# Causal attention in one core's four-stage kernel: head stacks written by transfers within SBUF, two heads' scores in two row halves of TensorE

## The chip, the cores and the metric

The kernel runs on one core of one Trainium2 chip. The metric is the device time of one execution in microseconds (us), lower is better. TensorE (PE) multiplies, VectorE (DVE), ScalarE (ACT) and GpSimd (POOL) do the element work, and SyncE (SP) issues most of the transfers, which 16 DMA engines carry out.

## The reference, cut to what matters

Four layers follow each other, each with a layer norm before it and another before its sum with the residual: a Mamba-2 scan, a ternary feed-forward network, causal attention, and a mixture of eight experts. `x` is (2, 512, 512). Only the attention is touched:

```python
B, L, D, H = (32, 64, 512, 32)      # H = 32 heads of 16; b, l, d come from x: 2, 512, 512
q = (x @ Wq.T + bq).reshape(b, l, h, hd).transpose(0, 2, 1, 3)
k = (x @ Wk.T + bk).reshape(b, l, h, hd).transpose(0, 2, 1, 3)
v = (x @ Wv.T + bv).reshape(b, l, h, hd).transpose(0, 2, 1, 3)
scores = jnp.einsum('bhqd,bhkd->bhqk', q, k) / math.sqrt(hd)
causal = jnp.tril(jnp.ones((l, l), bool))
scores = jnp.where(causal, scores, -jnp.inf)
att = jax.nn.softmax(scores, axis=-1)
out = jnp.einsum('bhqk,bhkd->bhqd', att, v)
return out.transpose(0, 2, 1, 3).reshape(b, l, d) @ Wo.T + bo
```

The kernel keeps the accuracy of float32 by splitting operands into a high and a low part and adding the products of the parts.

## The kernel before, in words

The attention's heads are taken in 16 *quads* of four heads of one sequence. A *pair of quads* m (0 to 7) shares one projection: 128 rows of Q and of K, which are 8 heads. A quad has 8 *units*: four blocks of 128 queries (qi) times two head pairs (p2); there are 128 units, numbered n, and n%16 is the place of a unit within m. In unit n

- PE makes the scores of two heads (j = 0, 1) in two PSUM banks (L1933), and adds the causal mask by a bf16 product behind each (L1934), then signals `s_ready`;
- DVE takes the negated maximum of each row (L1504, `nmax`), ACT the exponential (L1169, `prob`);
- two units later PE transposes the probabilities (L1943), and ACT (L1161) and DVE (L1514) copy one head each into `pA` or `pB`;
- every half quad PE multiplies them by V (L1908); DVE copies the result (L1520, `osb`), PE transposes it back (L1954), DVE divides by the sums (L1530).

Scores are one product each because the parts of Q and K are stacked along the contraction: for a head 16 rows each of Q's high, low, high, low part stand against K's high, high, low, low part, 64 rows in all. Before, these stacks are made by PE: a selection matrix `selz` spreads the rows of `qh` and `ql` (L1887, L1888), ACT copies the Q stack from PSUM (L1144, `qs`), DVE the K stack (L1493, `kst`). One stack of 128 rows holds two heads, so POOL writes K twice, each time with the other head's 64 rows zeroed (L874, `kz`, by `head`), and a head's score contracts over all 128 rows. `qs` and `kz` have two buffers, for even and odd quads.

These preparations for the next quads are cut into *pieces*, hung behind fixed units by the function `pieces`: behind n%16 = 5, 6, 8, 9 six projection products each (L360, Q then K; bank 7), after 6 and 9 ACT makes the high part `qh` (L1136) and DVE the low part `ql` (L1485), and one stack behind each of 11, 12, 13, 14, 0, 1, 2, 3. Each engine runs its own list in the order in which it is written, so all that stands behind a waiting instruction waits too. SP issues next to nothing meanwhile: the reloads of Q and K weights, three in all (L569, L570), and at the stage's end the expert weights (L577).

Of the kernel before, what the change touches and what calls it, by code (L numbers as in the profile page):

```python
# [57 lines left out]
def program(nc, hidden, w_conv, w_gate, w_dt, conv_w, conv_b, dt_bias, A_log, Dskip, norm_w, w_out,  # L58
            ff_gu, ff_dn, gate_s, up_s, down_s, wq, wk, bqk, wv, bv, wo, bo, gate_w, expert_w, out):
    ctx = ExitStack()  # L60
    with ctx:
# [119 lines left out]
        kst = sc("kst", [P, 2, L], F32R)  # L181
# [6 lines left out]
        kz = sc("kz", [P, 2, 2, 2, L], F32R)  # L188
# [6 lines left out]
        selz = sc("selz", [P, 4, 4, P], F32R)  # L195
        abv = sc("abv", [P, DM])
        futf = sc("futf", [P, P])
        fold = sc("fold", [P, 2, HD])
        spare = sc("spare", [P, 352 + 4 * DM])
# [4 lines left out]
        head = sc("head", [P, 2])  # L204
# [22 lines left out]
        def sd(name, shape, dt=F32):  # L227
# [65 lines left out]
        qk_ps, qk_h, qk_l, st_ps, st_k, st_q, kpad = (sem(s) for s in (  # L293
            "qk_ps", "qk_h", "qk_l", "st_ps", "st_k", "st_q", "kpad"))
# [140 lines left out]
        def pieces(n):  # L435

            m, s = n // 16, n % 16
            for at, what in ((0, ("k", 0, 1)), (1, ("k", 1, 1)), (2, ("q", 0, 1)), (3, ("q", 1, 1))):
                if s == at:
                    return (m,) + what  # L440
            for at, what in ((5, ("proj", 0, 0)), (6, ("proj", 0, 1)), (8, ("proj", 1, 0)), (9, ("proj", 1, 1)),
                             (11, ("k", 0, 0)), (12, ("k", 1, 0)), (13, ("q", 0, 0)), (14, ("q", 1, 0))):
                if s == at and m + 1 < AT * NB:
                    return (m + 1,) + what
            return None
# [17 lines left out]
        ORDER = (("k", 0), ("k", 1), ("q", 0), ("q", 1))  # L463
        SEL = 9 + 8 + 2 + 4 * 8
# [17 lines left out]
        def _(sp):  # L482
# [72 lines left out]
            if STAGES >= 3:  # L555
# [10 lines left out]
                with sp.Fori(0, AT - 1) as t:  # L566

                    sp.wait_ge(aq_lo, 2 * t + 2)
                    sp.dma_start(aqr[:, 0, :, :], wq[bass.ds(t + 1, 1)]).then_inc(aq_in, 16)  # L569
                    sp.dma_start(aqr[:, 1, :, :], wk[bass.ds(t + 1, 1)]).then_inc(aq_in, 16)  # L570
            if STAGES >= 4:
# [9 lines left out]
                sp.wait_ge(st_ps, 4 * QUADS)  # L581
# [123 lines left out]
        def _(pool):  # L705
# [96 lines left out]
            if STAGES >= 2:  # L802
                norm_wait(pool, 1, "tr", NT)
                pool.memset(acc[:, :, :], 0.0).then_inc(consts, 1)
                if STAGES >= 3:
# [25 lines left out]
                    flat = fold[:, :, :].rearrange("p a b -> p (a b)")  # L831
                    made(pool.tensor_tensor(flat, ident[:, 0:32], ident[:, 32:64], ALU.add))
                    made(pool.tensor_tensor(flat, flat, ident[:, 64:96], ALU.add))
                    made(pool.tensor_tensor(flat, flat, ident[:, 96:128], ALU.add))
# [25 lines left out]
            if STAGES >= 3:  # L860
# [7 lines left out]
                def padded(quad, p2):  # L868

                    pool.wait_ge(st_k, 2 * quad + p2 + 1)  # L870
                    if quad >= 2:
                        pool.wait_ge(s_ready, 8 * (quad - 1))
# [1220 lines left out]
```

## Time and profile before

| | us |
|---|---|
| median of 3 runs (1709.1 to 1710.33) | 1710.32 |
| profiled execution, its own time | 1712.04 |
| its span, first to last instruction | 1710.3 |
| PE busy over the span | 1549.1 (91%) |
| DVE / ACT / POOL busy | 1222.2 / 826.1 / 945.8 |
| mean granted TensorE clock | 0.962 |

A busy share is an average over four layers with different limits; what counts for a change in attention is read from its stretch, some 1218 to 1520 us from the span's start. Matmul durations in the rows include the pipeline: in a run of them the distance between two starts, 0.23 us for 512 columns, is what each costs, not the 0.39 us that stand beside it. "issue" names idle time in front of an instruction that waited for nothing visible.

### The profile page before, as it was taken

The page shows a single profiled execution, that of the slowest core. Times are in us where ns is not written, and L with a number is a line of the kernel's source. Part 1 is how long each engine was busy: PE and PEld are TensorE (multiplying, and loading weights), DVE is VectorE, ACT ScalarE, POOL GpSimd, SP SyncE. Part 2 cuts the span into 40 slices and gives each one's busy share as a digit, 9 for nine tenths or more (in the row PEclk, how much of TensorE's full clock was granted, in tenths as well). Part 3 has the DMA queues.
Part 4 walks back from the last instruction along what each step waited for, and adds up shares of the span by engine and source line. Part 5 has one row for each costly group of instructions (what it writes and reads, how often), then busy time and mean ns, then how long its engine had stood idle before and what let it go on. Part 6 is the DMA issues. An engine that isn't in the chain of part 4 may idle for free.

```text
span 1710.3 us, 26565 instructions
## 1 busy us (share of the span) xinstructions
PE 1549.1 (91%) x8870; PEld 1215.7 (71%) x8870; DVE 1222.2 (71%) x2024; ACT 826.1 (48%) x1639; POOL 945.8 (55%) x861
## 2 busy tenths in 40 slices
PE   5899999999999999999999879996899999987791
PEld 3677877878778778778787657874567767666681
DVE  5778788778778787877887866567466677767525
ACT  3464554554555545455554423331276666663231
POOL 4367576676675766776756851007442344327544
PEclk9999999999999999999999889998899999997796
DMA  3111012021110110211101111221000000032435
GB/s 119 38 50 59 17 50 64 12 79 38 48 61 18 49 61 12 80 37 49 61 19 50 56 56 62 74 99 37 1 14 1 14 1 1 28 146 75 133 133 166
DMA packets 49498, 92.61 MB, mean 54 GB/s; under 512 B 8016, under 2 KB 32720, under 8 KB 44176
## 3 DMA queue, kind: packets, MB, share of 16 engines
q1 hardware_dynamic: 45744, 79.58, 14.4%
q0 software_dynamic: 3680, 12.06, 2.1%
q8 instruction: 44, 0.72, 0.2%
q14 instruction: 30, 0.25, 0.0%
HBM read 81.14 MB, written 10.49 MB: 54 GB/s over the span
## 4 chain that ended last, share of the span: by engine, by line
PE 59%; DVE 17%; POOL 8%; issue 7%; ACT 6%; DMA 3%; SPq 0%; POOLq 0%; DVEq 0%; ACTq 0%
PE banks L360 28%; PE banks L1666 6%; DVE tap L1237 4%; PE banks L1943 3%; PE banks L1803 3%; PE banks L1731 2%; PE banks L1908 2%; PE banks L1725 2%; PE banks L1696 2%; DMA x<-in_w_gate 2%; PE banks L1933 2%; POOL wol L365 2%; PE banks L1740 2%; DVE xbc L1243 1%; DVE acc L629 1%
## 5 line engine op out<-in xcount | busy, mean ns | idle before, releaser
L1237 DVE SCALAR_TENSOR_TENSOR tap<-banks,parg,tap 128x511 f32<-128x511 f32 (+2 forms) x288 | 215.0, 747 | 26.9 <-ACT tap L943 19.6
L723 POOL TENSOR_TENSOR am<-ah,upto 128x1024 fp32r<-128x1024 f32 x64 | 121.6, 1901 | 179.7 <-PE banks L1696 138.6
L874 POOL TENSOR_SCALAR kz<-kst,head 128x512 fp32r<-128x512 f32 x64 | 99.0, 1564 | 160.3 <-DVE kst L1493 160.3
L360 PE MATMUL banks<-xTh,wch 128*128 128x512 f32 x384 | 162.8, 424 | 5.2 <-DVE em L1343 3.7
L951 ACT ACTIVATE th<-tap 128x512 f32<-128x512 f32 x96 | 60.7, 632 | 215.0 <-DVE tap L1237 212.9
L360 PE MATMUL banks<-xTh,wcl 128*128 128x512 f32 x384 | 151.2, 394 | 0.0
L360 PE MATMUL banks<-xTl,wch 128*128 128x512 f32 x384 | 150.7, 393 | 0.0
L1169 ACT ACTIVATE prob<-banks,nmax 128x128 f32<-128x128 f32 (+3 forms) x256 | 121.6, 529 | 55.3 <-DVE nmax L1504 55.1
L1504 DVE TENSOR_REDUCE nmax<-banks 128x2 f32<-128x256 f32 (+3 forms) x128 | 104.7, 818 | 40.5 <-PE banks L1934 40.3
L723 POOL TENSOR_TENSOR am<-al,upto 128x1024 fp32r<-128x1024 f32 x64 | 122.1, 1908 | 0.0
L1343 DVE TENSOR_TENSOR em<-banks,gmask 128x1024 f32<-128x1024 f32 x64 | 78.2, 1221 | 49.8 <-ACT banks L992 48.9
L360 PE MATMUL banks<-xTh,wgh 128*128 128x512 f32 x256 | 107.5, 420 | 0.9 <-DVE tap L1237 0.5
L1943 PE MATMUL banks<-ident,prob 128*128 128x128 f32 x640 | 95.9, 277 | 10.6 <-DVE pB L1514 7.2
L360 PE MATMUL banks<-woh,ynTh 128*128 128x512 f32 x256 | 103.3, 403 | 0.0
L360 PE MATMUL banks<-woh,ynTl 128*128 128x512 f32 x256 | 101.2, 395 | 0.0
L360 PE MATMUL banks<-wol,ynTh 128*128 128x512 f32 x256 | 100.9, 394 | 0.0
L360 PE MATMUL banks<-xTh,wgl 128*128 128x512 f32 x256 | 100.7, 394 | 0.0
L360 PE MATMUL banks<-xTl,wgh 128*128 128x512 f32 x256 | 100.0, 391 | 0.0
L360 PEld LDWEIGHTS banks<-xTh,wch 128*128 128x128 f32 x384 | 72.6, 189 | 34.2 <-DVE em L1343 10.0
L1666 PE MATMUL banks<-xTh,gu 128*128 128x512 f32 x224 | 89.9, 401 | 6.2 <-DVE hidf L1432 6.1
L943 ACT ACTIVATE tap<-banks,parg 128x512 f32<-128x512 f32 x96 | 74.1, 772 | 43.6 <-PE banks L360 37.0
L1243 DVE SCALAR_TENSOR_TENSOR xbc<-th,tap 128x512 f32<-128x512 f32 x96 | 86.5, 901 | 5.4 <-ACT th L951 0.9
(290 smaller groups left out, 4393.1 us busy)
## 6 DMA issues: line engine op xcount, KB each, us to landing
x<-grownT SPq DMA_DIRECT2D x96, 128.0 KB, 4.8
x<-in_w_conv SPq DMA_DIRECT2D x7, 1536.0 KB, 6.5
x<-in_w_gate SPq DMA_DIRECT2D x8, 1024.0 KB, 4.9
x<-in_w_out SPq DMA_DIRECT2D x8, 1024.0 KB, 4.8
eraw<-in_expert_w SPq DMA_DIRECT2D x8, 1024.0 KB, 7.3
gur<-in_ff_gu SPq DMA_DIRECT2D x7, 1024.0 KB, 4.7
x<-in_hidden SPq DMA_DIRECT2D x16, 256.0 KB, 3.6
mates<-yd SPq DMA_DIRECT2D x8, 512.0 KB, 4.6
```

The costliest lines, as they stand in the source:

```text
L360: m = nc.tensor.matmul(o, a, b, start=first and n == 0, stop=last and n == len(terms) - 1)
L723: m = pool.tensor_tensor(am[:, part, :, :], a[:, i, :].bitcast(F32).unsqueeze(2).to_broadcast([P, HG, P]), upto[:, :].unsqueeze(1).to_broa ...
L874: m = pool.tensor_scalar(kz[:, quad % 2, p2, j, :], kst[:, p2, :].bitcast(F32), head[:, j:j + 1], None, ALU.mult)
L943: nc.scalar.activation(tap[:, q % 2, :], bk(CONV_BANKS[q % 2]), ACT.Identity, bias=parg[:, CT * KC + q:CT * KC + q + 1], scale=parg[:, KC ...
L951: nc.scalar.activation(th[:, :], tap[:, q % 2, :], ACT.Tanh).then_inc(tanh_ready, 1)
L1169: e = nc.scalar.activation(prob[:, n % 2, j, 0:kw], bk(2 * (n % 2) + j)[:, 0:kw], ACT.Exp, bias=nmax[:, n % 2, j:j + 1])
L1237: nc.vector.scalar_tensor_tensor(tap[:, q % 2, sh:L], bk(CONV_BANKS[q % 2])[:, 0:L - sh], parg[:, KC * q + k:KC * q + k + 1], tap[:, q % 2 ...
L1243: nc.vector.scalar_tensor_tensor(xbc[:, q, b * L:(b + 1) * L], th[:, :], 1.0, tap[:, q % 2, :], ALU.add, ALU.mult).then_inc(xbc_ready, 1)
L1343: nc.vector.tensor_tensor(em[:, s % 2, :, :], decayed, gmask[:, :].unsqueeze(1).to_broadcast([P, HG, P]), ALU.mult).then_inc(m_ready, 1)
L1504: nc.vector.tensor_reduce(nmax[:, n % 2, :], banks[:, 2 * (n % 2):2 * (n % 2) + 2, 0:kw], AX, ALU.max, negate=True).then_inc(max_ready, 1)
L1666: m = mat(bk(2 * w + ft), gu[:, k, ft, w, :], part[:, k, tok], start=(k == 0 and part is xTh), stop=(k == KT - 1 and part is xTl))
L1943: m = pe.transpose(bk(4 + j)[:, c * P:(c + 1) * P], prob[:, w % 2, j, c * P:(c + 1) * P], ident[:, :])
```

## The change

The stacks are no longer made on PE, ACT, DVE and POOL. SP writes them by transfers within SBUF: a transfer copies 16 rows of 512 float32 (32 KB) of `qh` or `ql` to their place in `qs` or `kz`. A quad needs 2 (Q, K) x 2 (p2) x 4 (parts) x 2 (heads) = 32 of them, all 16 quads 512. `kz` has no zeroed half; a score contracts over 64 rows, head j over rows 64j to 64j+63 of the array, the two heads' products stand next to each other, and the two mask products stand behind both. Since no selection matrix scales Q any more, ACT scales the Q weights and bias (`q_scaled`). The projections are cut into 8 pieces of 3 products, behind n%16 = 3 to 6 and 8 to 11. Two new waits hold the buffers: PE waits at a quad's first unit for `qk_in`, and ACT waits before it overwrites `qh` for all transfers of the pair of quads before.

```diff
         def pieces(n):
             m, s = n // 16, n % 16
-            for at, what in ((0, ("k", 0, 1)), (1, ("k", 1, 1)), (2, ("q", 0, 1)), (3, ("q", 1, 1))):
...
+            for w, at in ((0, (3, 4, 5, 6)), (1, (8, 9, 10, 11))):
+                if s in at and m + 1 < AT * NB:
+                    return m + 1, w, at.index(s)
...
-        SEL = 9 + 8 + 2 + 4 * 8
+        SEL = 9 + 4
+        STACK = 2 * 2 * 4 * 2
+        def stacked(quad):
+            return 16 * STACK * (quad // 2 + 1)
...
+                for m in range(AT * NB):
+                    for u in range(2):
+                        quad = 2 * m + u
+                        if quad >= 2:
+                            sp.wait_ge(s_ready, 8 * (quad - 1))
+                        for w in range(2):
+                            sp.wait_ge(qk_l, 2 * m + w + 1)
+                            for p2 in range(2):
+                                of = 32 * (2 * u + p2)
+                                for r, part in enumerate((qh, ql, qh, ql) if w == 0 else (qh, qh, ql, ql)):
+                                    for j in range(2):
+                                        row, at = of + HD * j, 64 * j + HD * r
+                                        sp.dma_start((qs, kz)[w][at:at + HD, quad % 2, p2, :].bitcast(F32),
+                                                     part[row:row + HD, w, :].bitcast(F32)).then_inc(qk_in[quad % 2], 16)
+                    t = m // NB
+                    if m % NB == 0 and t + 1 < AT:
+                        sp.wait_ge(aq_lo, 2 * t + 2)
+                        sp.dma_start(aqr[:, 0, :, :], wq[t + 1]).then_inc(aq_in, 16)
...
                 sp.wait_ge(v_f, NT)
-                sp.wait_ge(st_ps, 4 * QUADS)
+                for n in range(2):
+                    sp.wait_ge(qk_in[n], stacked(QUADS - 2 + n))
...
-                def padded(quad, p2):
-                    pool.wait_ge(st_k, 2 * quad + p2 + 1)
...
+                    nc.scalar.activation(aqr[:, 0, :, :], aqr[:, 0, :, :], ACT.Copy, scale=HD ** -0.5).then_inc(q_scaled, 1)
+                    act.wait_ge(q_scaled, t + 1 + (t > 0))
...
                 def high(m, w):
                     act.wait_ge(qk_ps, 2 * m + w + 1)
+                    if m:
+                        for u in range(2):
+                            act.wait_ge(qk_in[u], stacked(2 * (m - 1) + u))
...
-                def queries(quad, p2):
-                    act.wait_ge(st_ps, 4 * quad + 2 + p2 + 1)
...
-                def keys(quad, p2):
-                    dve.wait_ge(st_ps, 4 * quad + p2 + 1)
...
-                            pe.wait_ge(kpad, 2 * quad + 2)
-                            pe.wait_ge(st_q, 2 * quad + 2)
+                            pe.wait_ge(qk_in[quad % 2], stacked(quad))
...
                         for j in range(2):
-                            o = bk(2 * (n % 2) + j)
-                            kn = max(kw, 2 * P)
-                            mat(o[:, 0:kn], qs[:, quad % 2, p2, qi * P:kw], kz[:, quad % 2, p2, j, 0:kn], start=True, stop=False)
-                            m = mat(o[:, kw - P:kw], identb[:, :], future[:, :], start=False, stop=True)
+                            rows, kn = slice(64 * j, 64 * j + 64), max(kw, 2 * P)
+                            mat(bk(2 * (n % 2) + j)[:, 0:kn], qs[rows, quad % 2, p2, qi * P:kw], kz[rows, quad % 2, p2, 0:kn],
+                                start=True, stop=False)
+                        for j in range(2):
+                            m = mat(bk(2 * (n % 2) + j)[:, kw - P:kw], identb[:, :], future[:, :], start=False, stop=True)
```

Also gone are POOL's 38 small instructions that built `selz`, `fold` and `head` during the feed-forward layer.

In the list of SP after the change, the transfers of an even quad from the second pair of quads on (names: `qs` the Q stack, `kz` the K stack; x4 is four in a row):

```order
L576 DMA qs<-qh 16x512 [waits qk_l,s_ready]
L576 DMA qs<-qh 16x512
L576 DMA qs<-ql 16x512 x2
L576 DMA qs<-qh 16x512 x2
L576 DMA qs<-ql 16x512 x2
L576 DMA qs<-qh 16x512 x2
L576 DMA qs<-ql 16x512 x2
L576 DMA qs<-qh 16x512 x2
L576 DMA qs<-ql 16x512 x2
L576 DMA kz<-qh 16x512 [waits qk_l]
```

Fifteen more K transfers follow, then the odd quad's 32, all from the same `qh` and `ql`. Before, SP has nothing at this place.

On PE, a unit with the projection piece behind it (n%16 = 9), before:

```order
L1933 MATMUL banks<-kz,qs 128x256 [waits exp_ready]
L1934 MATMUL banks<-future,identb 128x128
L1933 MATMUL banks<-kz,qs 128x256
L1934 MATMUL banks<-future,identb 128x128
L1943 MATMUL banks<-ident,prob 128x128 [waits pt_a,exp_ready]
L1943 MATMUL banks<-ident,prob 128x128 x3
L1943 MATMUL banks<-ident,prob 128x128 [waits pt_v]
L1943 MATMUL banks<-ident,prob 128x128 x3
L360 MATMUL banks<-xTh,aqh 128x512
L360 MATMUL banks<-xTl,aqh 128x512
L360 MATMUL banks<-xTh,aql 128x512
```

and the same unit after:

```order
L1877 MATMUL banks<-kz,qs 128x256 [waits exp_ready]
L1877 MATMUL banks<-kz,qs 128x256
L1880 MATMUL banks<-future,identb 128x128 x2
L1889 MATMUL banks<-ident,prob 128x128 [waits pt_a,exp_ready]
L1889 MATMUL banks<-ident,prob 128x128 x3
L1889 MATMUL banks<-ident,prob 128x128 [waits pt_v]
L1889 MATMUL banks<-ident,prob 128x128 x3
L358 MATMUL banks<-xTh,aqh 128x512
L358 MATMUL banks<-xTl,aqh 128x512
L358 MATMUL banks<-xTh,aql 128x512
```

The masks moved behind the pair of scores, and three products follow where six did before (the other three of the six rows' worth stand behind another unit).

On ACT, around the high part of Q's next projection (n%16 = 6), after the change:

```order
L1150 ACTIVATE prob<-banks,nmax 128x512 [waits pt_ps,max_ready]
L1150 ACTIVATE prob<-banks,nmax 128x512 [waits pt_ps]
L1124 ACTIVATE qh<-banks,abqk 128x512 [waits qk_in1,qk_in0,qk_ps]
L1142 COPY pB<-banks 128x384 [waits pt_ps]
L1150 ACTIVATE prob<-banks,nmax 128x512 [waits pt_ps,max_ready]
```

Before, the third row is `L1136 ACTIVATE qh<-banks,abqk 128x512 [waits qk_ps]` at the same place; its wait has gained the transfers of both quads, and the copies and exponentials of the units stand behind it.

## Rows read from the trace of the kernel before

**Rows 1.** Busy time by stretch: us, busy (instructions) of each engine, clock, DMA share, GB/s.

```profile
1260.00:1295.00 35.00, 32.97 (x283) 24.28 (x281) 24.49 (x43) 23.97 (x54) 14.88 (x10) 1.00 0.05 16
```

**Rows 2.** ACT's high parts in the timeline: start us, us, engine, line, op, tiles.

```profile
1284.99 0.69 ACT L1136 ACTIVATE qh<-banks,abqk 128x512 fp32r<-128x512 f32 x1 [0.50 <-PE banks L360]
...
1463.97 0.69 ACT L1136 ACTIVATE qh<-banks,abqk 128x512 fp32r<-128x512 f32 x1 [0.50 <-PE banks L360]
```

**Rows 3.** Timeline of PE: a stack (0.57 us to the next start), and a unit's scores.

```profile
1302.59 0.50 PE L1887 MATMUL banks<-qh,selz 128*128 128x512 f32 x1
...
1303.16 0.39 PE L1933 MATMUL banks<-kz,qs 128*128 128x512 f32 x1
...
1316.70 0.40 PE L1933 MATMUL banks<-kz,qs 128*128 128x512 f32 x1
...
1316.94 0.23 PE L1934 MATMUL banks<-future,identb 128*128 128x128 bf16 x1
...
1316.98 0.48 PE L1933 MATMUL banks<-kz,qs 128*128 128x512 f32 x1
...
1317.37 0.82 PE L1943 MATMUL banks<-ident,prob 128*128 128x128 f32 x6
```

**Rows 4.** SP's transfers in the timeline: start us, us that SP was in it.

```profile
6.76 0.68 SPq L489 DMA_DIRECT2D par<-in_conv_w  x1
...
1138.17 0.43 SPq L562 DMA_DIRECT2D abo<-in_bo  x1
1138.65 0.45 SPq L563 DMA_DIRECT2D rw<-in_gate_w  x1
...
1271.50 0.33 SPq L569 DMA_DIRECT2D aqr<-in_wq  x1
1271.93 0.38 SPq L570 DMA_DIRECT2D aqr<-in_wk  x1
```

**Rows 5.** DMA issues of the page: tiles, count, KB each, median us from issue to landing.

```profile
xnd<-acc SPq DMA_DIRECT2D x8, 256.0 KB, 2.0
...
gus<-in_gate_s SPq DMA_DIRECT2D x1, 7.0 KB, 2.7
```

**Rows 6.** Timeline, odd quad's units 8 to 12: what leads to K's low part.

```profile
1250.02 0.36 PE L1933 MATMUL banks<-kz,qs 128*128 128x256 f32 x1
...
1255.21 0.48 PE L360 MATMUL banks<-xTh,aqh 128*128 128x512 f32 x1
...
1256.68 0.28 PE L1933 MATMUL banks<-kz,qs 128*128 128x256 f32 x1
...
1257.61 0.75 DVE L1485 SCALAR_TENSOR_TENSOR ql<-banks,abqk,qh 128x512 fp32r<-128x512 f32 x1 [1.42 <-ACT qh L1136]
...
1260.32 0.34 PE L1933 MATMUL banks<-kz,qs 128*128 128x384 f32 x1
```

**Rows 7.** Timeline of the first quad's start.

```profile
1220.28 0.75 DVE L1485 SCALAR_TENSOR_TENSOR ql<-banks,abqk,qh 128x512 fp32r<-128x512 f32 x1 [2.85 <-ACT qh L1136]
...
1224.88 0.75 DVE L1485 SCALAR_TENSOR_TENSOR ql<-banks,abqk,qh 128x512 fp32r<-128x512 f32 x1 [3.85 <-ACT qh L1136]
...
1233.71 0.55 PE L1933 MATMUL banks<-kz,qs 128*128 128x256 f32 x1 [2.36 <-POOL kz L874]
```

**Rows 8.** PE's weight loads where the tile's shape changes, in the timeline.

```profile
1318.12 0.59 PEld L1908 LDWEIGHTS banks<-pA,v 128*32 128x32 f32 x16 [0.17 <-issue]
...
1318.90 0.19 PEld L360 LDWEIGHTS banks<-xTh,aqh 128*128 128x128 f32 x1 [0.20 <-issue]
```

**Rows 9.** Busy time by stretch around the first quad's start, columns as in group 1.

```profile
1228.00:1230.00 2.00, 0.73 (x2) 0.30 (x2) 0.67 (x1) 0.51 (x1) 2.00 (x2) 0.89 0.00 0
1230.00:1232.00 2.00, 1.22 (x2) 0.50 (x2) 0.00 (x0) 0.66 (x2) 2.00 (x3) 0.50 0.00 0
...
1239.00:1240.00 1.00, 1.00 (x6) 0.64 (x4) 0.55 (x2) 0.76 (x3) 1.00 (x2) 0.60 0.00 0
```

**Rows 10.** The page's busy tenths of POOL in 40 slices of 42.8 us.

```profile
POOL 4367576676675766776756851007442344327544
```

More of the change, by code:

```diff
@@ L187, in program @@
         future = sc("future", [P, P], BF16)
-        kz = sc("kz", [P, 2, 2, 2, L], F32R)
+        kz = sc("kz", [P, 2, 2, L], F32R)
+        under_aqr = sc("under_aqr", [P, 2, 2, L])
         aqr = sc("aqr", [P, 2, KT, P])
@@ L866, in _ @@
                     low(pool, awl[:, k, :], awr[:, k, :], awh[:, k, :]).then_inc(aw_lo, 1)
-                def padded(quad, p2):
-                    pool.wait_ge(st_k, 2 * quad + p2 + 1)
-                    if quad >= 2:
-                        pool.wait_ge(s_ready, 8 * (quad - 1))
-                    for j in range(2):
-                        m = pool.tensor_scalar(kz[:, quad % 2, p2, j, :], kst[:, p2, :].bitcast(F32), head[:, j:j + 1],
-                                               None, ALU.mult)
-                    m.then_inc(kpad, 1)
-                for p2 in range(2):
-                    padded(0, p2)
                 for n in range(UNITS):
-                    piece = pieces(n)
-                    if piece and piece[1] == "k":
-                        padded(2 * piece[0] + piece[3], piece[2])
                     if n % 32 == 14 and n // 32 + 1 < AT:
@@ L1173, in _ @@
                         if piece:
-                            m, what, i, u = piece
-                            if what == "proj" and u == 1:
-                                high(m, i)
-                            if what == "q":
-                                queries(2 * m + u, i)
+                            m, w, part = piece
+                            if part == KT - 1:
+                                high(m, w)
                         if n % 32 == 14 and n // 32 + 1 < AT:
@@ L1535, in _ @@
                     if piece:
-                        m, what, i, u = piece
-                        if what == "proj" and u == 1:
-                            lows(m, i)
-                        if what == "k":
-                            keys(2 * m + u, i)
+                        m, w, part = piece
+                        if part == KT - 1:
+                            lows(m, w)
                 dve.wait_ge(wide_in, 32)
@@ L1914, in _ @@
                 for w in range(2):
-                    for part in range(2):
+                    for part in range(KT):
                         project(0, w, part)
-                for what, i in ORDER:
-                    stack(0, what, i, 0)
                 pe.wait_ge(v_f, NT)
@@ L1957, in _ @@
                     if piece:
-                        prepare(*piece)
+                        project(*piece)
                 for i in range(NT + 6):
```

75 lines of the change are left out of this document (11 added, 64 removed).

## The prediction, made before the changed kernel ran

> **What bounds the kernel now.** I read the busy time by stretch first. In the steady part of attention PE is busy 33.0 of 35 us at full clock, DVE and ACT some 24, POOL 15, and the transfers run at 16 GB/s [rows 1]: PE sets the pace and the transfer side is empty. Then the timeline, for the rhythm: the high part of Q's projection for m = 2 starts at 1284.99, that for m = 7 at 1463.97, so a pair of quads takes 178.98 / 5 = 35.8 us [rows 2], a unit 2.24. Last the list of transfers, because the change puts 512 instructions on an engine, SP, that issues next to none in this stage.
>
> **What goes.** A stack costs PE 0.57 us from its first start to the next instruction's [rows 3]. There are 64, so 8 x 0.57 = 4.6 us per pair of quads: were PE still the bound, a pair would take 31.2 us and the stage would lose 64 x 0.57 = 36 us. ACT's and DVE's 32 copies each and POOL's 64 multiplications go too; all three engines have room [rows 1], so I count these at nothing. The projection products stay 24 per pair, only spread.
>
> **What the transfers cost.** SP is in a transfer 0.43 to 0.45 us and starts the next 0.48 us later when they stand in a row (1138.17 to 1138.65); two in a loop start 0.43 apart; the first after a wait takes 0.33, and patterns with more dimensions 0.68 [rows 4]. None of these is 16 rows within SBUF. The new ones have the plainest pattern and stand in a row, so I take 0.47 and keep 0.33 and 0.68 as ends. A quad is then 32 x 0.47 = 15.0 us of issuing. To landing the nearest rows are 2.0 us for a transfer out of SBUF and 2.7 for 7 KB into it [rows 5]; I take 2.0 (bounds 1.5, a quarter below the nearest row, and 2.7). SP's mean load is thus 30 of 35.8 us, which would fit. What doesn't fit is the chain that the waits make:
>
> 1. The odd quad's last transfer lands. Only then may its first unit start, and only then may ACT write the next `qh`, in front of its copies and exponentials.
> 2. From the odd quad's first score to K's next low part. Before, units 8 to 12 take 1250.02 to 1260.32, 10.3 us [rows 6]; two pieces of six products (1.47 each, 1255.21 to 1256.68) and a stack leave them, four pieces of three (about 0.77 each) come, which gives about 10.0. ACT and DVE first do the held-up high and low part of Q (0.69 + 0.75, and their queues behind), 1.5 us. Behind unit 11's piece come high and low part of K: from the end of the piece at 1256.68 the same two took until 1258.36, 1.7 us [rows 6]. Sum 13.2. The even quad's 16 Q transfers (7.5 us, from about 1.5 us on) lie under this.
> 3. Then 48 transfers in a row, 16 of K for the even quad and 32 for the odd one: 48 x 0.47 = 22.6 us. The even quad runs beneath, and starts some us late.
> 4. Landing, 2.0 us, and the circle closes.
>
> That is 13.2 + 22.6 + 2.0 = 37.8 us per pair against 35.8, or 2.0 more. PE's 4.6 us are gone from its work and come back as waiting at the first unit of each even quad. There are 7 such circles: +14.0.
>
> **The start.** Q's first low part ends at 1221.03 [rows 7]. From there 32 transfers are issued without a gap (K's low part is ready at 1225.6, before its turn), to 1236.1, and land at 1238.1; the first score stood at 1233.71, behind POOL's padding [rows 7]. The odd quad lands 15.0 later, at 1253.1, where it began at 1250.02 [rows 6]: +3.1 at the point where the circles begin.
>
> **The score products.** Before, scores and masks of a unit with 512 columns take 0.67 us of PE: 0.24 to the mask, 0.04 to the second score, 0.39 from there to the end of its mask [rows 3]. If the two half-height products run at the same time, the second's own 0.32 goes. If the array must first empty when the tile's shape changes, each unit pays twice what weight loads pay where the shape changes now, 0.17 and 0.20 [rows 8]: with both, 0.72; with the emptying alone, 1.04. No row shows a product over 64 rows, so the bounds are -0.32 and +0.37 per unit, and I take +0.05, overlap and emptying, the value that uses both rows. On the path are only the four units of step 2, so 28 units: +1.4, bounds -9 and +10. (The Trainium skill, TensorEngine Tiling (Array Packing), Key Properties, speaks for and against: tiles run in parallel, and "Changing tiling mode (not just tile) drains the TensorE". By the first alone the sum would be some 9 us less, by the second alone 10 more. The 0.17 and 0.20 us agree with the second; no run here shows the first.)
>
> **The rest.** ACT's scaling of 128x512 (about 0.6) stands once in the feed-forward layer, at most +0.6, and three times where SP is what everybody waits for; taken as 0. The 38 small instructions on POOL go from the feed-forward layer, where POOL is busy a tenth of the time and less in slices 25 to 27 [rows 10]: 0. The expert loads wait for quad 15's landing in place of the last stack; that lies a whole quad, about 15 us, before the attention's end, time enough for the first five. SP's reloads of Q and K weights fall where it waits for `s_ready`.
>
> **Sum.** 14.0 + 3.1 + 1.4 = 18.5, on the profiled execution's own 1712.0: 1730.5. That execution is 1.7 above the median of the runs, 1710.3, so the median goes to about 1729, and I say 1730.
>
> **Rivals.**
> A, the transfers are hidden after all: faster. The place is step 3. The circle is 48c + 15.2 with c the time of an issue; it equals 35.8 at c = 0.43, and with the start's cost the whole breaks even at about 0.42. At c = 0.33, the row after a wait, it is 31.0, and PE's 31.2 rules: 7 x -4.6, with all 64 stacks -36, 1675; at c = 0.40 (34.4) it is 7 x -1.4, -1.4 at the start and +1.4 for the scores, 1701. For it: 16 rows may be quicker to issue than 128. Against: 16 KB (L563) and 256 KB (L562) took SP 0.45 and 0.43 [rows 4], so size hardly matters.
> B, the clock falls. After a sparse stretch (0.73 of 2 us busy) the granted clock went from 1 to 0.50, the 1.2 GHz level, and in 1239 to 1240 it was still at 0.60 on average, with PE busy all of it [rows 9]. The change puts a wait of some 4 us and thin units before each even quad. If PE then works 4 us at half clock each time, the even quad, whose 15 us of issuing have hardly any slack over PE's work, ends 2 us later: 7 x 2 = +14, 1744. For it: the same kind of gap did it once. Against: it needs the even quad on the path, and step 3 says SP is. (The Trainium skill, TensorE: Matmul & The Clock Gate, Part 1, has it that idleness throttles the clock to half and only renewed activity frees it; rows 9 agree. By that rule the time would be 1744.)
> C, an issue costs 0.68 as with the longer patterns: the circle is 32.6 + 15.2 = 47.8, +12.0 each, 84, and 64 x 0.21 = 13 more at the start: 1812 with the start's 3.1 and the scores' 1.4. For it: 512 unrolled issues in a row are unlike anything here. Against: the 0.68 rows have patterns with many short runs.
> D, the half-height products don't run side by side: that is the +10 bound, 1739, within the forecast's range.
>
> **Chances and range.** Forecast with D 0.58, B 0.22, C 0.08, A 0.12. A change below 0.2% of the time, 3.4 us, is what a measurement here can't tell from none. An issue of 0.44 to 0.50 moves the forecast by (7 x 48 + 64) x 0.03 = 12 us either way, the landing by -4 to +5, the scores by -9 to +10. Faster comes from A (0.10 of its 0.12), same from the low edge of the forecast and A's rest, 0.08, slower 0.82. For 8 in 10 I go from 1706 to 1772: B with a slow issue is in, C and most of A are out.
>
> **What would show it.** In the changed profile: SP starts its transfers 0.47 apart, 48 without a gap, and idles some 4 us before the even quad's K transfers; PE's first score of even quads waits for a DMA some 4 us; ACT's `qh` for Q waits for a DMA; those starts are 37.8 us apart; the second score of a unit starts well under 0.2 us behind the first, with about 0.2 idle around the pair. Wrong would be: PE without waits for transfers (A), clock 0.50 behind each even start (B), starts 0.68 apart (C). If the landing takes far over 2 us with a queue that is never empty, step 4 is what I have mis-sized.

## The result and the profile after

| | before | after |
|---|---|---|
| median (runs) | 1709.72 us (4) | 1814.03 us (4; 1806.01 to 1815.37) |
| profiled execution, its own time | 1712.04 | 1815.37 |
| span | 1710.3 | 1813.6 |
| ratio after / before | | 1.061, 95% interval 1.059 to 1.062 |

The change costs 104 us. The forecast was 1730 in a range of 1706 to 1772: right in its sign, wrong in its size. In the steady part of attention, PE was busy 33 of 35 us [rows 1]. The same stretch after (columns as in group 1), and then a line of the page of after: where the chain that ended last spent its time, by engine.

```profile
1260.00:1295.00 35.00, 27.57 (x200) 18.30 (x200) 17.09 (x29) 18.25 (x41) 2.49 (x2) 0.74 0.22 56
```

```profile
PE 49%; SPq 14%; DVE 13%; issue 7%; POOL 7%; ACT 5%; DMA 4%; POOLq 0%; ACTq 0%; DVEq 0%
```

Every engine that computes is less busy. SPq, SyncE inside its issuing instructions, is now 14% of the chain, where before SP had next to nothing to do in attention. All of these 14% are on one line, L576, the stack transfers. The page's group for the scores (idle time in front of them behind the last bar) and its row for a transfer name what PE waits for:

```profile
L1877 PE MATMUL banks<-kz,qs 64*128 64x256 f32 (+2 forms) x256 | 63.3, 491 | 91.9 <-DMA kz<-ql 89.2
...
qs<-qh SPq DMA_DIRECT2D x128, 32.0 KB, 2.0
```

89.2 us of waiting for the last K transfer, at 16 quad starts. The rhythm, against [rows 2], is in ACT's high parts (timeline: start, duration, instruction, idle time before it):

```profile
1260.43 0.69 ACT L1124 ACTIVATE qh<-banks,abqk 128x512 fp32r<-128x512 f32 x1 [6.91 <-DMA kz<-ql]
...
1309.22 0.69 ACT L1124 ACTIVATE qh<-banks,abqk 128x512 fp32r<-128x512 f32 x1 [5.64 <-DMA kz<-ql]
...
1552.14 0.69 ACT L1124 ACTIVATE qh<-banks,abqk 128x512 fp32r<-128x512 f32 x1 [4.37 <-DMA kz<-ql]
```

A pair of quads takes (1552.14 - 1260.43) / 6 = 48.6 us instead of 35.8, and the high part of Q waits for the transfers each time. The seven circles run from the odd quad's start at 1260.37 to the last odd quad's at 1600.57, 340.2 us; before, the same starts are 1250.02 [rows 6] and 1498.39, 248.4 us (timeline of PE, first before, then after):

```profile
1498.39 0.36 PE L1933 MATMUL banks<-kz,qs 128*128 128x256 f32 x1
```

```profile
1260.37 0.58 PE L1877 MATMUL banks<-kz,qs 64*128 64x256 f32 x2 [5.75 <-DMA kz<-ql]
...
1600.57 0.58 PE L1877 MATMUL banks<-kz,qs 64*128 64x256 f32 x2 [5.61 <-DMA kz<-ql]
```

That is 91.8 us for the circles, 10.4 for the later start, and 1.1 behind the last odd quad's start: 103.3, the whole difference of the spans.

One circle as the chain of waits tells it (start, us, what; the runs of SPq rows are cut):

```profile
1307.17 1.95 DMA kz<-ql
1309.22 0.70 ACT qh L1124
1309.94 0.75 DVE ql L1464
1310.70 1.13 DVE nmax L1474
1312.35 1.12 PE banks L1889 x4
1313.46 1.28 PE banks L358 x3
...
1323.39 0.76 DVE ql L1464
...
1324.72 0.59 SPq L576
...
1331.04 1.50 SPq L576
...
1355.76 1.94 DMA kz<-ql
1357.80 0.70 ACT qh L1124
```

It is the circle of the prediction, link by link: the odd quad's last landing lets Q's high part go, units 8 to 11 follow, then K's low part, then SP alone from 1324.17 to 1356.34, and the last landing. And SP's timeline in it (x4 is four transfers in a row):

```profile
1324.17 2.40 SPq L576 DMA_DIRECT2D kz<-qh  x4
1326.62 2.49 SPq L576 DMA_DIRECT2D kz<-ql  x4
1329.14 3.40 SPq L576 DMA_DIRECT2D kz<-qh  x4
...
1345.28 3.47 SPq L576 DMA_DIRECT2D kz<-qh  x4
...
1353.85 2.49 SPq L576 DMA_DIRECT2D kz<-ql  x4
```

Four transfers take 2.52 us from start to start (1326.62 to 1329.14), 0.63 each, where I had taken 0.47; and two of these groups are 0.9 us longer than the others.

### The profile page after: what moved, and what is told of

It is laid out like the page before. It is cut to its first block, busy times and chain, and to the rows that moved or that the text cites. A ratio compares the mean times of both kernels' runs of the same rounds, so it can differ in the third digit from the quotient of the medians.

```text
span 1813.6 us, 26583 instructions
## 1 busy us (share of the span) xinstructions
PE 1565.7 (86%) x8742; PEld 1206.3 (67%) x8742; DVE 1202.6 (66%) x1992; ACT 817.3 (45%) x1612; POOL 834.1 (46%) x759
## 4 chain that ended last, share of the span: by engine, by line
PE 49%; SPq 14%; DVE 13%; issue 7%; POOL 7%; ACT 5%; DMA 4%; POOLq 0%; ACTq 0%; DVEq 0%
PE banks L358 26%; SPq L576 14%; PE banks L1634 6%; DVE tap L1216 3%; PE banks L1771 3%; PE banks L1699 2%; PE banks L1693 2%; PE banks L1664 2%; DMA x<-in_w_gate 2%; POOL wol L363 2%; PE banks L1708 1%; DVE acc L642 1%; PE banks L1889 1%; POOL am L736 1%; DVE xbc L1222 1%
## 5 line engine op out<-in xcount | busy, mean ns | idle before, releaser
L1877 PE MATMUL banks<-kz,qs 64*128 64x256 f32 (+2 forms) x256 | 63.3, 491 | 91.9 <-DMA kz<-ql 89.2
L1889 PE MATMUL banks<-ident,prob 128*128 128x128 f32 x640 | 125.5, 333 | 18.3 <-DVE pA L1484 7.1
L363 POOL TENSOR_TENSOR aql<-aqr,aqh 128x512 fp32r<-128x512 f32 x8 | 10.0, 1273 | 252.1 <-ACT aqh L1076 252.1
L1877 PEld LDWEIGHTS banks<-kz,qs 64*128 64x128 f32 x256 | 28.1, 216 | 132.9 <-DMA kz<-ql 74.1
L1889 PEld LDWEIGHTS banks<-ident,prob 128*128 128x128 f32 x640 | 90.8, 175 | 27.9 <-DVE pA L1484 11.0
```

Source lines behind the costliest of these rows:

```text
L1877: mat(bk(2 * (n % 2) + j)[:, 0:kn], qs[rows, quad % 2, p2, qi * P:kw], kz[rows, quad % 2, p2, 0:kn], start=True, stop=False)
L1889: m = pe.transpose(bk(4 + j)[:, c * P:(c + 1) * P], prob[:, w % 2, j, c * P:(c + 1) * P], ident[:, :])
```

## Experiments

Two theories stood at first. *Issue*: SP's time per transfer sets the 48.6 us. *Clock*: the granted clock is 0.50 for some us around each quad's start (0.74 on the mean of 1260 to 1295), and PE, not SP, is late.

**m1_bursts. What an issue costs, by itself.** The kernel before, with bursts on SP where nobody waits for it:

```diff
+                for n in range(N):
+                    sp.dma_start(to[0][16 * (n % 8):16 * (n % 8) + 16, :] if n < 8 else to[1][16 * (n % 8):16 * (n % 8) + 16, :],
+                                 abo[16 * (n % 8):16 * (n % 8) + 16, :]).then_inc(wide_in, 16)
+                sp.wait_ge(wide_in, 32 + 16 * N * 1)
...
+                for n in range(N):
+                    sp.dma_start(to[n // 8][16 * (n % 8):16 * (n % 8) + 16, :],
+                                 hidden[16 * n:16 * n + 16, :]).then_inc(wide_in, 16)
```

N is 12, and each burst waits for the one before. The bursts are 16 x 512 within SBUF, 128 x 64 within SBUF, 16 x 512 from HBM, 32 x 512 within SBUF, 128 x 64 from HBM.

> The kernel before, with five bursts of 12 transfers on SP in the attention stage, where SP has nothing to do; each burst waits until the one before has landed. Bursts in order: (a) 16 rows x 512 within SBUF, (b) 128 rows x 64 within SBUF, (c) 16 rows x 512 from HBM, (d) 32 rows x 512 within SBUF, (e) 128 rows x 64 from HBM. Theory 1, the source decides: a transfer with both sides in SBUF costs SP 0.63 us, as in the changed kernel, and one from HBM 0.47 as in the rows of before: (a), (b), (d) 0.63, (c), (e) 0.47. Theory 2, the shape decides, 16 rows cost more than 128: (a), (c) 0.63, (b), (e) 0.47, (d) between. Theory 3, it is the long run of transfers and neither: all five 0.47. The time of the kernel stays at 1710 by all of them, unless the traffic within SBUF slows the engines.

Ratio 1.000 (0.999 to 1.001). SP's timeline of the five bursts, in their order:

```profile
1340.77 7.57 SPq L574 DMA_DIRECT2D spare<-abo  x12
1349.71 8.81 SPq L578 DMA_DIRECT2D spare<-abo  x12
1359.77 5.50 SPq L582 DMA_DIRECT2D spare<-in_hidden  x12
1366.68 8.09 SPq L586 DMA_DIRECT2D spare<-abo  x12
1376.17 5.57 SPq L590 DMA_DIRECT2D spare<-in_hidden  x12
```

7.57 / 12 = 0.63 us for the transfer of the change. The second and the fourth burst look dearer only because each holds one long issue (1.79 and 1.15 us, more on these below); their other transfers start 0.64 and 0.63 apart. The same shape from HBM takes 0.46, as my rows did [rows 4]: all of those came from HBM. Neither height nor size decides.

All five bursts end in SBUF, so m1 alone would allow "the source" as the cause. The kernel before has transfers out of SBUF into HBM, each right behind a wait:

```profile
1541.41 0.33 SPq L594 DMA_DIRECT2D xnd<-acc  x1
```

0.33 us is what one from HBM takes behind a wait [rows 4], while one within SBUF takes 0.51 to 0.59 there (after). So it is having both ends in SBUF that costs, not the source alone.

**m2_half. Half the issues.** One transfer of 32 rows for both heads, 16 per quad (the scores then mix the two heads' parts and are wrong; number and shapes of all products stay).

```diff
-                                    for j in range(2):
-                                        row, at = of + HD * j, 64 * j + HD * r
-                                        sp.dma_start((qs, kz)[w][at:at + HD, quad % 2, p2, :].bitcast(F32),
-                                                     part[row:row + HD, w, :].bitcast(F32)).then_inc(qk_in[quad % 2], 16)
+                                    sp.dma_start((qs, kz)[w][32 * r:32 * r + 32, quad % 2, p2, :].bitcast(F32),
+                                                 part[of:of + 32, w, :].bitcast(F32)).then_inc(qk_in[quad % 2], 16)
```

> The changed kernel with half the transfers: 32 neighbouring rows (both heads) go in one, 16 per quad instead of 32, the same bytes. The rows of the stacks stand in another order, so the scores are those of mixed heads; the work is the same. Theory A, the time lies in the number of issues on SP and in the chain of waits that they stand in: the circle is 24 x 0.65 + 2.0 + 13.2 = 30.8 us per pair of quads, less than PE's 31.2 + 0.4, so PE sets the pace again: -4.2 us per pair against before, 8 x -4.2 = -34, some 1677 (1670 to 1692). Theory B, the time lies in the bytes within SBUF or in the landing: 64 KB take twice as long, nothing is won, 1800 or more.

1695.29 us, ratio 0.992 (0.990 to 0.994): 119 us faster than after, and 14 faster than before. The bytes are the same, so the number of issues is the cause of the loss. But it isn't the 1677 that PE's bound of 31.2 us per pair promised.

**m3_qh2. `qh` and `ql` twice**, so that the high part doesn't wait for the transfers of the pair before it.

```diff
-                    if m:
+                    if m > 1:
                         for u in range(2):
-                            act.wait_ge(qk_in[u], stacked(2 * (m - 1) + u))
+                            act.wait_ge(qk_in[u], stacked(2 * (m - 2) + u))
```

> The changed kernel with two buffers of qh and ql by turns, so that ACT waits for the transfers of the pair of quads before the last only. All 32 transfers per quad stay. Theory A (chain): the closed circle of 48.6 us per pair opens, and what is left is SP's own load, 64 x 0.63 + 2.7 for the longer ones = 43.0 us: 7 x -5.6 = -39, some 1775. Theory B (SP's load alone sets the pace already, the wait of ACT costs nothing): no change, 1814.

1795.37 us, ratio 1.050 (1.047 to 1.052), a miss by 20. ACT's high parts of Q, four pairs apart:

```profile
1302.01 0.69 ACT L1126 ACTIVATE qhs<-banks,abqk 128x512 fp32r<-128x512 f32 x1
...
1486.76 0.69 ACT L1126 ACTIVATE qhs<-banks,abqk 128x512 fp32r<-128x512 f32 x1
```

46.2 us per pair: 64 issues of 0.63 are 40.3, SP still waits 3.4 per pair for K's low part (24.0 us in seven waits), its long issues add 1.7, and the weights' reloads are most of the rest. With the circle opened SP's plain load remains above 35.8: two buffers don't save this change.

**m4_warm and m14_warm2. The clock.** The kernel after, with products that nobody reads ahead of the wait at a quad's start (20; then 24), and in the second kernel 6 more within the odd quad's first unit.

```diff
+                            if n:
+                                for i in range(20):
+                                    mat(bk(2 * (n % 2) + i % 2), awh[:, i % KT, 0:P], xTh[:, i % KT, 0:L], start=True, stop=True)
                             pe.wait_ge(qk_in[quad % 2], stacked(quad))
```

```diff
+                            if j and n % 16 == 8 and n // 16 + 1 < AT * NB:
+                                pe.wait_ge(qk_l, 2 * (n // 16) + 3)
+                                for i in range(6):
+                                    mat(bk(7), awh[:, i % KT, 0:P], xTh[:, i % KT, 0:L], start=True, stop=True)
```

> The changed kernel with 20 products of 512 columns (some 4.3 us at full clock) into the unit's own score banks in front of PE's wait for the transfers at each quad's start but the first; they are overwritten by the scores. Theory A, the clock that falls in the waits (0.50 for some 8 us after each quad's start) is part of the loss: the clock stays at 1, the way from the odd quad's start to K's low part falls from 15.0 to 13.2 us, 7 x -1.8 = -13, some 1801. Theory B, the slow stretches lie beside SP's issuing and cost nothing: 1814 within 3.

> The kernel after with products whose result nobody reads, in two places: 24 before the wait at each quad's start, and 6 in the odd quad's first unit between the transposes of its two heads, where TensorE idled 1.3 us in the run with 20 fillers and its clock then fell to 0.50, the 1.2 GHz level, until some 3 us later. So that run had only moved the fall, not removed it. The unit's work of about 3.3 us at half clock lies on the way from the odd quad's start to K's transfers, 13.4 us then. If the half clock there costs what it seems, this way shortens by 1.3 to 1.6 us, seven times, and the time is 1801 us (1797 to 1804). If that stretch waits for ScalarE's and VectorE's held-up work and not for TensorE, the time stays at 1808 to 1812 us.

The first: 1810.79 us, ratio 1.059 (1.055 to 1.062), no different from after, by which I held the clock to be harmless. That was wrong. Its trace has the fall two microseconds later, in the idle time of the odd quad's first unit; the second kernel fills that too. Windows (columns as in group 1) of after, of m4 and of m14, in an odd quad's first unit:

```profile
1311.00:1313.00 2.00, 1.17 (x6) 0.77 (x5) 1.62 (x3) 1.14 (x2) 0.00 (x0) 0.50 0.14 33
```

```profile
1312.00:1314.00 2.00, 2.00 (x8) 1.25 (x7) 0.69 (x1) 1.46 (x4) 0.00 (x0) 0.50 0.23 53
```

```profile
1314.00:1316.00 2.00, 2.00 (x12) 1.49 (x11) 1.58 (x4) 1.37 (x3) 0.00 (x0) 1.00 0.17 41
```

The second: 1800.22 us, ratio 1.051 (1.050 to 1.053), 13.8 less than after. From Q's high part at the odd quad's start to K's high part it takes 11.9 us each time; in after it is 13.4 to 14.7, 14.1 on average:

```profile
1311.99 0.69 ACT L1124 ACTIVATE qh<-banks,abqk 128x512 fp32r<-128x512 f32 x1 [5.80 <-DMA kz<-ql]
1323.91 0.69 ACT L1124 ACTIVATE qh<-banks,abqk 128x512 fp32r<-128x512 f32 x1
```

So the fall to 0.50, the 1.2 GHz level, costs 2.1 us per circle, 15 us in all. (The layers ahead took 4.5 us longer in the profiled execution of m14 than in that of after; from Q's first low part to the last score, attention alone, it is 379.5 us against 396.4.) The clock's cost lies in the link where SP waits for K's projection. At the even quads it falls as well, but there the transfers are what is late.

**m5_scores. Only the scores.** The kernel before, with the half-height products side by side; stacks still by PE, no padding on POOL.

```diff
                         for j in range(2):
-                            mat(o[:, 0:kn], qs[:, quad % 2, p2, qi * P:kw], kz[:, quad % 2, p2, j, 0:kn], start=True, stop=False)
-                            m = mat(o[:, kw - P:kw], identb[:, :], future[:, :], start=False, stop=True)
+                            mat(bk(2 * (n % 2) + j)[:, 0:kn], qs[rows, quad % 2, p2, qi * P:kw], kz[rows, quad % 2, p2, 0:kn],
+                                start=True, stop=False)
+                        for j in range(2):
+                            m = mat(bk(2 * (n % 2) + j)[:, kw - P:kw], identb[:, :], future[:, :], start=False, stop=True)
```

> The kernel before with only its scores changed: the two heads' products on 64 rows each side by side and the masks behind them; the stacks are still made on TensorE, and VectorE copies K's stack where GpSimd made two padded ones. The price in the prediction (+0.05 us per unit, 64 units on both halves) gives 1704 to 1716 us. The half-transfer run showed 0.17 to 0.37 us of idle TensorE ahead of each pair of 64-row products against 0.107 us for 256 columns that no longer run one behind the other; if that idle time is the price of changing from 128 rows to 64 and back, this kernel is slower, about +0.1 us per unit, 1718 to 1728 us. If it only takes the place of a wait for exp that was there anyway, 1704 to 1712 us.

1708.99 us, ratio 1.000 (0.999 to 1.001). Q's high parts four pairs apart:

```profile
1245.73 0.69 ACT L1132 ACTIVATE qh<-banks,abqk 128x512 fp32r<-128x512 f32 x1 [0.51 <-PE banks L361]
...
1390.72 0.69 ACT L1132 ACTIVATE qh<-banks,abqk 128x512 fp32r<-128x512 f32 x1 [0.51 <-PE banks L361]
```

36.25 us per pair against 35.8, so 0.03 us per unit; in return the first score stands 11.1 us behind Q's first low part instead of 12.7, since K need not be padded. Two small effects that cancel. The 0.03 is not of the scores alone, as POOL's and DVE's part in K's stack changed with them. That the products do run at the same time is seen in after at full clock: the way from a pair's start to its masks grows with the columns of one product.

```profile
1303.29 0.51 PE L1877 MATMUL banks<-kz,qs 64*128 64x512 f32 x2
1303.73 0.29 PE L1880 MATMUL banks<-future,identb 128*128 128x128 bf16 x2
...
1317.27 0.38 PE L1877 MATMUL banks<-kz,qs 64*128 64x256 f32 x2
1317.58 0.29 PE L1880 MATMUL banks<-future,identb 128*128 128x128 bf16 x2
```

0.31 us for 256 columns, 0.44 for 512: 0.13 more for 256 columns in each of two products, where 256 columns of one alone cost 0.115 (half of 0.23) and two in a row would cost 0.23. What this saves comes back as idle time: in four pairs of m5 the weight loads ahead of 65 score pairs stand idle 17.0 us without a visible cause, 0.26 each, mostly 0.17 or 0.36, which fits the 0.17 and 0.20 of [rows 8] and their sum. That this is the emptying of the array is the reading that fits, no run separates it from other causes. (The Trainium skill, TensorEngine Tiling (Array Packing), Key Properties, states both, the tiles in parallel and the drain at a change of mode; the traces agree with both, and here they are worth the same.)

**m8_every4. Half the issues, heads not mixed.** A head's contraction rows may stand in any order that Q and K share. With part r on every fourth partition from r on, one transfer of 32 rows serves both heads.

```diff
+                                    sp.dma_start((qs, kz)[w][r:P:4, quad % 2, p2, :].bitcast(F32),
+                                                 part[of:of + 32, w, :].bitcast(F32)).then_inc(qk_in[quad % 2], 16)
```

> The kernel after with the contraction rows of a head in another order: part r of both heads goes to every fourth partition from r on, in one transfer of 32 rows where there were two of 16. Q and K have the same order, so the scores are those of the reference. 16 transfers per quad. If what costs is the number of issues, this is the half-transfer run again: 1695 us (1692 to 1699), 0.63 us per issue. If partitions four apart cost more in a transfer (descriptors or landing), SyncE's issue goes over 0.63 us or the landing over 2.0 us, and at 0.8 us per issue it would still be 1700 us or below, as SyncE then has 25.6 us of 34.7 us per pair; only landings over 4 us would show.

1699.42 us, ratio 0.995 (0.993 to 0.996); 0.4 above the range that m2 led me to expect. An issue takes SP 0.59 us as before, the landing is 2.1 instead of 2.0: partitions four apart cost next to nothing.

Here the other half of the story shows. PE has no stacks, SP is hidden, and still a pair takes 34.8 us, 1.4 less than m5 and not 4.6. Groups of PE over four pairs, of m5 (145.0 us) and of m8 (139.2 us); the last column is the idle time before them:

```profile
L1940 PE MATMUL banks<-ident,prob 128*128 128x128 f32 x320 | 47.2, 275 | 5.0 <-DVE pB L1510 3.5 <-ACT pB L1157 1.3
L1928 PE MATMUL banks<-kz,qs 64*128 64x256 f32 (+2 forms) x130 | 27.8, 424 | 0.0
L1883 PE MATMUL banks<-qh,selz 128*128 128x512 f32 x32 | 15.6, 488 | 1.7 <-DVE kz L1489 1.7
L361 PE MATMUL banks<-xTh,aqh 128*128 128x512 f32 x32 | 14.0, 436 | 0.0
```

```profile
L1887 PE MATMUL banks<-ident,prob 128*128 128x128 f32 x322 | 51.0, 282 | 9.0 <-DVE pA L1482 4.0 <-DVE pB L1482 3.8 <-ACT pB L1140 0.6
L1875 PE MATMUL banks<-kz,qs 64*128 64x256 f32 (+2 forms) x128 | 28.0, 434 | 3.1 <-DMA kz<-ql 1.6 <-ACT prob L1148 1.4
L358 PE MATMUL banks<-xTh,aqh 128*128 128x512 f32 x32 | 15.4, 483 | 0.0
```

The 32 stacks are worth 32 x 0.57 + 1.7 = 19.9 us. Back come 4.0 of waits of the transposes for the copies of `pA` and `pB`, 3.8 in which they run longer, 3.1 of waits for K and the exponential, and 1.4 in the first product of a projection, probably because eight small pieces have twice as many starts as four: 12.3 of the 14.1 that are missing. A part is the clock: in these four pairs of m8 it is at 0.50 twice (one of the two below), in m5 never, 6.8 us of PE at half pace and so 3.4 us at most, spread over these groups and others.

```profile
1294.90:1298.30 3.40, 3.40 (x27) 2.15 (x26) 1.88 (x3) 2.03 (x5) 0.00 (x0) 0.51 0.34 84
```

The stacks had stood in time that PE would partly have waited.

**m11_qonly and m13_earlyk. One part alone.** The kernel before with only Q's stacks by transfers (8 per quad, four partitions apart), K by PE and POOL, scores over 128 rows; the projections come in eight pieces, as in after. The first has K's first stacks behind units 13 and 14, the second behind 11 and 12 as before had them.

```diff
-                return m + 1, "k", s - 13, 0
+                return m + 1, "k", s - 11, 0
```

> The kernel before with one part changed: Q's stacks come by 8 transfers of 32 rows per quad, K's are still made on TensorE and padded on GpSimd, and the scores are products over 128 rows as before. SyncE has 16 x 0.63 = 10.1 us per pair, hidden. TensorE loses 4 stacks of 0.57 us per pair, 2.3 us, ScalarE four copies. If TensorE is what bounds, 33.5 us per pair and 1693 us (1690 to 1697). If the chain of a unit (scores, maximum, exp, transposes, copies) had begun to bound as in the half-transfer run, half of it: 1702 us.

> The kernel with only Q's stacks by transfers, with K's two first stacks of a pair two steps earlier (11 and 12), where the kernel before has them. Its first form waited 24.8 us in 7 waits for GpSimd's padded stacks at the even quads, and nothing else in it was late. If these waits are all that made it 1732 us, this is 1707 us (1703 to 1710), about the time of before, although TensorE has four stacks of 0.57 us less in each pair: then the stacks removed are no longer on the path to the end. If TensorE's work is the bound, 1693 us. If the waits go on at another place, over 1715 us.

The first: 1732.12 us, ratio 1.013 (1.012 to 1.015). 39 above what TensorE's work gave. I had moved K's stacks two units later without asking who stands behind them. PE waits, all waits of 1240 to 1560 for one line:

```profile
PE banks L1942 <- POOL kz L893: 24.8, 7, 3.6
```

POOL needs 3.1 us for a padded stack, and the even quad's first score is behind it. The second: 1696.17 us, ratio 0.992 (0.990 to 0.993), the fastest here with the reference's scores. It gains 36 us where the waits were 24.8, so they were not all that made the first slow. The other 11 were not taken apart; the clock is a likely part, with a mean of 0.95 from 1240 to 1500 in the first and 1.00 from 1240 to 1480 in the second:

```profile
1308.00:1314.00 6.00, 5.37 (x23) 4.69 (x24) 2.23 (x4) 1.22 (x3) 1.40 (x2) 0.50 0.47 131
```

That row is of the first, behind one of its waits. ACT's high parts in the second, four pairs apart:

```profile
1279.47 0.69 ACT L1158 ACTIVATE qh<-banks,abqk 128x512 fp32r<-128x512 f32 x1
...
1416.65 0.69 ACT L1158 ACTIVATE qh<-banks,abqk 128x512 fp32r<-128x512 f32 x1
```

That is 34.3 us per pair; four stacks less give 1.5 us, where TensorE as the only bound would give 2.3; if the eight pieces cost here the 0.35 per pair that they did in m8 (1.4 in four), half of the difference is theirs. Neither of my two numbers, 1707 and 1693, was met, the second nearly.

**m7_pool and m12_poolk. Another engine issues.** m7 is m3 with K's 8 low parts of a quad issued by POOL; m12 is m8 with all of K's 8.

```diff
+                            pool.dma_start(kz[r:P:4, quad % 2, p2, :].bitcast(F32),
+                                           part[of:of + 32, 1, :].bitcast(F32)).then_inc(k_in, 16)
```

> The kernel with qh and ql double-buffered, all transfers of 16 rows as in after, but K's low parts, 8 of 32 per quad, issued by GpSimd. If SyncE's issue time bounds, it goes from 40.3 to 24 x 2 x 0.63 = 30.2 us per pair, below the 34.7 us that the half-transfer run needed: 1695 to 1710 us, given that GpSimd issues one in about 0.95 us (7.6 us per quad). If the queue or the landing of many small transfers bounds and not the issuing engine, the time stays near the 1795 us of the double-buffered run. If an issue on GpSimd takes over 2 us, 16 per pair take over 32 us and it is over 1710 us.

> The kernel with partitions four apart (16 transfers of 32 rows per quad), but K's 8 are issued by GpSimd. In the run with K's low parts on GpSimd an issue took it 0.49 us (SyncE 0.59 and a gap of 0.05). What is left to gain are the waits of TensorE for kz, 3.1 us in four pairs with those for exp, so 0.4 us per pair for kz: 3 us, and 0.7 us at the first quad: 1696 us (1693 to 1699). If GpSimd's issues delay each other or land later than SyncE's, TensorE waits more for kz than 0.4 us per pair and the time is over 1700 us.

m7: 1715.30 us, ratio 1.004 (1.003 to 1.006), 5 above the range. A quarter of the transfers off SP, all 16 rows high, takes 80 us from m3's time. The landing stays at 2.0 us in both, so nothing piled up in the queue. It is the issuing engine that bounded, not the DMA engines or the landing of many small transfers. m12: 1700.78 us, ratio 0.994 (0.992 to 0.996), no different from m8 and just in the range of "delayed"; PE still waits for the last K transfer, 3.8 us in five waits to 1480.

Both pay behind attention for what GpSimd did in it: from the last score to the end it is 201 us in both, and 197.3 to 197.5 in m2, m8 and m13. GpSimd's first gather of the expert layer (`xg`) takes 2.5 us instead of 1.5, and PE waits longer for it. PE's waits for it behind attention (us, times, longest) in m8 and in m12:

```profile
PE banks L1962 <- DMA xg<-xnd,row_from: 6.6, 2, 6.2
```

```profile
PE banks L1977 <- DMA xg<-xnd,row_from: 10.5, 2, 10.2
```

Of the 14.7 us between the profiled executions of m7 and m8, 3.8 are this, 5.2 come before the first score, 3.8 from there to the last odd quad, and the rest lies ahead of attention and behind its last odd quad. In m12 attention alone is 4.0 shorter than in m8, though not by the waits for K, and these 3.7 us cancel it. Why a gather that follows plain transfers of GpSimd starts so, no run shows.

## Why the prediction was wrong

*Step "What the transfers cost", c = 0.47 us: wrong, and the main cause.* It is 0.63 (after and m1). By the forecast's own formula, (7 x 48 + 64) x 0.16 = 64 us. I drew both ends from rows whose transfers came from HBM, and wrote that none of them was a transfer within SBUF; then I let size and pattern decide the value within them. The upper end, 0.68, was near the truth, and rival C with it came to 1812 for a probability of 0.08. Its place and its arithmetic held, the odds didn't.

*Step 3, "48 transfers in a row": right in mechanism, 22.6 us measured as 31.5 on average (32.2 in the circle shown).* 30.3 are c. The rest are issues of 1.0 to 1.7 us instead of 0.6, two in the circle above; in the trace of after there are 15 of them in 512, and they cost the seven circles 9 us. They are not at fixed places of SP's list: counted from 0 they are 155, 179 and 207 in after and 141, 164 and 183 in m4, whose SP list is the same. What stands beside every one of the 15 is a packet of 16 KB of the queue that the profile calls `instruction` (1330.85 to 1332.18 and 1347.00 to 1348.37 in the circle shown). Around the second, queue, kind, packets, MB and share in 1345.28 to 1348.70:

```profile
q8 instruction: 1, 0.02, 2.5%
```

It is so for 107 of the 108 long issues of all the experiments and after, and only one of the 16 such packets in after's attention meets no long issue. That the packet is the cause is likely by this; no run changed it.

*Step 2, 13.2 us: right, but for the clock.* Measured 15.0 in the circle shown and 15.6 on average; with the clock held (m14), 11.9 + 1.5 = 13.4. The forecast had the held-up high part and missed that its own idle time would halve the clock for the units behind it. Rival B named the cause, gave 14 us as its price and put it at the even quads, behind the wait of PE; it cost 15 at the odd ones. That its number came so near is luck. I had it as an alternative to the forecast, while it adds to it. (The Trainium skill, TensorE: Matmul & The Clock Gate, Part 1, says that idleness throttles the clock; m14, 13.8 us faster by work that nobody reads, agrees.)

*Step 4, 2.0 us: counted a little double.* A landing counts from the start of the issue, which the 48 x c had in it already: last issue's end to the odd quad's start is 1.4. That gives back 0.6 eight times, 5 us in all.

*The start, +3.1: measured +10.4*, c again (64 x 0.16 = 10), less the double count and SP's start at 1218.50 where I had 1221.03 (the layers ahead took that much less in this execution).

Sum of the corrections: 64 for c, 9 for the long issues, 17 for step 2 (7 x 2.4, of which 15 the clock), -5 for the landings, -2.5 for SP's earlier start, 2 because the seven pairs of before took 35.5 on average and not 35.8 (the last has no projections to make), -1.4 for the scores, which step 2 as measured contains, and 1 behind the last odd quad's start: 84. The spans ask for 103.3 - 18.5 = 84.8.

*The score products, +0.05 us per unit: right.* The overlap and the idle time taken for emptying are both there, and m5 has +0.03.

*What goes: 31.2 us per pair as PE's bound: wrong, without effect on the forecast.* With stacks gone and transfers hidden it is 34.8 (m8). Rival A's 1675 was never to be had; the gain at hidden transfers is 10 us (m8) to 14 (m2), not 35. I took PE's busy share for the whole pace and didn't ask what the unit's chain over ACT and DVE would allow once PE had less to do.

*The chances.* Rivals B and C were not exclusive of the forecast but terms of it, both costly on the same side. A range built by asking which single one holds ended at 1772.

## What to carry to other kernels

Price an issue from a row with the same kind of source and destination, and where the profile has none, give the whole spread of the rows the weight, above all if the answer turns on it: here break-even was 0.42 us and the nearest rows ran from 0.33 to 0.68. When work moves to transfers, count instructions of the issuing engine first, and choose the layout so that one transfer carries several pieces: any order of contraction rows will do if both operands have it. And a busy engine relieved of work gives back only what nothing else holds; ask which wait each removed instruction was covering.

## What the hardware showed

- An issue on SyncE takes 0.63 us from start to start within SBUF, for 16 and 32 rows, 0.64 for 128, and 0.46 to 0.47 from HBM (m1). Behind a wait SyncE is in one 0.51 to 0.59 us within SBUF (after), 0.33 from HBM and 0.33 out of SBUF into HBM (before). GpSimd is in one 0.49 us (16 rows, m7) or 0.53 (32 rows, m12), within SBUF.
- 32 KB within SBUF land 2.0 us after the start of the issue on 16 partitions and 1.8 on 128, 64 KB 2.0 on 32 adjacent ones (m1) and 2.1 on every fourth (m8).
- In after 15 of 512 issues on SyncE, written out one by one, take 0.4 to 1.1 us longer, each beside a 16 KB packet of the instruction queue.
- In m7 and m12, where GpSimd had issued 128 plain transfers, its first gather afterwards takes 2.5 us against 1.5 in m8, and what follows attention 3.7 us longer.
- Two products over 64 rows each run side by side (0.13 us for 256 columns more in both), and idle time of 0.26 us per pair, with the change of shape, takes this back up to 512 columns (m5).
- In m4 TensorE was busy until 1307.6, then idle for 0.84, 0.66 and 1.30 us between short pieces, and its clock was at 0.50 from 1312 to 1314, with PE busy all of it. Filling the idle time there as well gave 14 us back (m14 against after), although the products added are over 90 us of PE at full clock.
